# A transformer layer's value projection: its second phase moved behind the fourth pair of the step, a weighting product in its old place

## What is computed

```python
q, k, v = proj(Wq, bq), proj(Wk, bk), proj(Wv, bv)        # (B, 16, S, 16), v as 256 features
q = _apply_rope(q, cos, sin) * scale
k = _apply_rope(k, cos, sin)
attn = jax.nn.softmax(jnp.einsum('bhsd,bhtd->bhst', q, k), axis=-1)
out = jnp.einsum('bhst,bhtd->bhsd', attn, v)
x = _layernorm(x + out @ Wo.T + bo)
h = jax.nn.relu(x @ Wq1.T + b1)                           # Wq1, Wq2 in {-1, 0, 1}
x = _layernorm(x + h @ Wq2.T + b2)
```

## Time and profile before

| | us |
|---|---|
| median of 3 runs | 3234.84 (3234.15 to 3235.83) |
| the profiled execution | 3235.67 |
| its span, first to last instruction | 3233.9 |
| TensorE busy | 3190.5 |
| VectorE busy | 2970.8 |
| ScalarE busy | 2528.2 |
| GpSimd busy | 2157.4 |
| mean granted TensorE clock | 0.991 |

### The profile page before, as it was taken

How to read it: one execution, slowest core, us unless ns; L and a number is a source line. 1 busy time by engine, 2 the same in 40 slices (tenths; PEclk the granted TensorE clock), 3 DMA queues, 4 the chain that set the end, 5 groups by cost and what they waited for, 6 DMA issues and landing times.

```text
span 3233.9 us, 82328 instructions
## 1 busy us (share of the span) xinstructions
PE 3190.5 (99%) x31110; PEld 1769.4 (55%) x31110; DVE 2970.8 (92%) x5710; ACT 2528.2 (78%) x4963; POOL 2157.4 (67%) x2457
## 2 busy tenths in 40 slices
PE   6999999999999999999999999999999999999998
PEld 4545555555555555555555555555555555555555
DVE  7989999999999999999999999999999999999993
ACT  3878888878888888878878877888878878877774
POOL 2676766766766766766767767767767667664455
PEclk7999999999999999999999999999999999999999
DMA  8445354454354454454454454454453453453411
GB/s 214 115 102 110 92 118 106 99 118 110 94 119 107 98 119 105 100 119 99 103 119 103 100 119 102 103 119 100 105 119 96 106 121 91 111 110 73 97 57 35
DMA packets 312712, 342.02 MB, mean 106 GB/s; under 512 B 77372, under 2 KB 259964, under 8 KB 312316
## 3 DMA queue, kind: packets, MB, share of 16 engines
q1 hardware_dynamic: 311740, 335.97, 45.5%
q10 hardware_dynamic: 576, 0.79, 0.2%
HBM read 196.41 MB, written 140.24 MB: 104 GB/s over the span
## 4 chain that ended last, share of the span: by engine, by line
PE 97%; DMA 1%; ACT 1%; DVE 1%; issue 0%; SPq 0%; POOL 0%; ACTq 0%; POOLq 0%; DVEq 0%
PE ob L1049 31%; PE sc L1031 27%; PE job L787 26%; PE ms L1019 11%; PE job L838 0%; ACT prob L1187 0%; PE ms L895 0%; DVE mxp L1619 0%; PE sc L787 0%; DMA qa<-qk_parts 0%; SPq L482 0%; ACT at_st L1194 0%; DMA maxima<-nm 0%; DMA attention<-at_st 0%; DMA os_<-wv 0%
## 5 line engine op out<-in xcount | busy, mean ns | idle before, releaser
L1367 DVE TENSOR_REDUCE mxp<-ms 128x1 f32<-128x512 f32 x4064 | 2602.2, 680 | 193.3 <-PE ms L1019 155.8
L1187 ACT ACTIVATE prob<-sc 128x512 f32<-128x512 f32 x4096 | 2224.9, 597 | 593.7 <-PE sc L1031 562.0
L1019 PE MATMUL ms<-ka,qa 48*128 48x512 f32 x4064 | 1494.4, 440 | 3.3 <-DVE mxp L1619 2.2
L1031 PE MATMUL sc<-qa,ka 50*128 50x512 f32 x4096 | 1495.0, 438 | 2.2 <-ACT prob L1187 0.8
L1031 PEld LDWEIGHTS sc<-qa,ka 50*128 50x128 f32 x4096 | 694.3, 184 | 1020.9 <-ACT prob L1187 862.4
L1049 PE MATMUL ob<-prob,v_sb 128*17 128x512 f32 (+1 forms) x8528 | 1087.3, 582 | 4.5 <-ACT at_st L1194 4.2
L1019 PEld LDWEIGHTS ms<-ka,qa 48*128 48x128 f32 x4064 | 692.7, 184 | 11.7 <-DVE mxp L1367 5.2
L1735 POOL TENSOR_TENSOR ve<-mv,eps_sb 128x2 f32<-128x2 f32 x123 | 24.1, 196 | 571.9 <-DVE mv L1394 571.9
L1756 POOL TENSOR_TENSOR hid_r<-hid,hid_r 128x512 fp32r<-128x512 f32 x248 | 319.6, 1289 | 19.8
L1049 PEld LDWEIGHTS ob<-prob,v_sb 128*17 128x17 f32 x8528 | 141.4, 95 | 314.1 <-issue 314.0
L787 PEld LDWEIGHTS job<-h_t,w_sb 64*128 64x128 f32 x3968 | 271.4, 185 | 17.8 <-issue 1.6
(11 more groups left out here) (251 smaller groups left out, 2740.4 us busy)
## 6 DMA issues: line engine op xcount, KB each, us to landing
qk_parts<-parts SPq DMA_DIRECT2D x122, 512.0 KB, 4.3
ka<-qk_parts SPq DMA_DIRECT2D x378, 128.0 KB, 4.7
qa<-qk_parts SPq DMA_DIRECT2D x378, 128.0 KB, 7.3
attention<-at_st SPq DMA_DIRECT2D x127, 256.0 KB, 4.1
v_sb<-v_ones SPq DMA_DIRECT2D x68, 272.0 KB, 8.4
v_ones<-v_st SPq DMA_DIRECT2D x64, 272.0 KB, 2.4
xn<-x SPq DMA_DIRECT2D x63, 256.0 KB, 4.7
out<-y SPq DMA_DIRECT2D x63, 256.0 KB, 3.9
```

What stands on the lines that cost most here:

```text
L1019: nc.tensor.matmul(ms[upto(b, g, NS1, at) % MS_BANKS][:, :], operand(qa, b, unit_, j, ROWS)[:, qt * P:(qt + 1) * P], operand(ka, b, unit_, ...
L1031: nc.tensor.matmul(sc[upto(b, g, HG * STEPS, n) % SC_BANKS][:, :], operand(ka, b, unit_, j, ROWS + MROWS)[:, tt * P:(tt + 1) * P], operand ...
L1187: nc.scalar.activation(prob[st_ % 2][:, j, :], sc[upto(b, g, HG * STEPS, n) % SC_BANKS][:, :], ACT.Exp).then_inc(s["exp_done"], 1)
L1367: nc.vector.reduce_max(mxp[(b * G + g) % 2][:, kh, j * TT + qt:j * TT + qt + 1], ms[upto(b, g, NS1, at) % MS_BANKS][:, :], AX.X).then_inc( ...
```

## The change

`"v1"` joins the tuple of jobs that stand behind the fourth pair. So TensorE issues the product of the step before behind the second pair, and `v1` behind the fourth. ScalarE's copy of `v1` goes from between the second and third exponential to behind the fourth, and VectorE's copy from behind the second maximum to behind the third.

```diff
-JOBS_BEHIND = ("e0", "o0", "v0", "t3a", "f0", "f2", "g0", "g2")
+JOBS_BEHIND = ("e0", "o0", "v0", "v1", "t3a", "f0", "f2", "g0", "g2")
...
                         for job_ in jobs_at(b, g, st_, tail):
-                            finish(job_)
+                            if job_[2] != "v1":
+                                finish(job_)
...
                         for job_ in jobs_at(b, g, st_, tail):
+                            if job_[2] == "v1":
+                                finish(job_)
                             finish_rest(job_)
...
-                                if stage == "proj" and part == 1:
+                                if stage == "proj" and part == (2 if name == "v1" else 1):
                                     take_key_half(*at, name)
```

## The result

| | before | changed |
|---|---|---|
| median of 7 runs, us | 3235.01 (3234.15 to 3236.9) | 3245.57 (3243.6 to 3249.24) |
| the profiled execution, us | 3235.67 | 3249.24 |
| its span, us | 3233.9 | 3247.4 |
| mean granted TensorE clock | 0.991 | 0.991 |

The changed kernel is slower: ratio 1.0032, 95% interval 1.0022 to 1.0041, 10.6 us between the medians. 3245.7 us was predicted, 3238 to 3252 as the range. The profiled execution of the changed kernel is the slowest of its seven, so its span is 13.5 us longer where the medians differ by 10.6. I therefore compare steps, which repeat, and not ends.

What follows compares the result with a forecast made beforehand. TensorE, busy 99%, was taken to bound the kernel, held up by ScalarE's exponential latency. 8.6 + 1.0 + 1.3 = 10.9 us on 3235.67 gave 3246.6; less 0.8 for the median, 3245.7 us, range 3238 to 3252.

Steps and rivals of the forecast that it cites:

- Steps 7 and 8: TensorE's two steps with `v1` and `f0`: 3.09 and 3.32 us, together 6.41 us against 6.25 before.
- All eight distances: Starts between pairs: step 7 0.40, 1.41, 0.34, 0.94 us; step 8 0.39, 1.41, 0.34, 1.18 us.
- 0.16 us per unit: Extra time of steps 7 and 8 in each of 54 units, 8.6 us in all.
- The copies cost nothing: ScalarE's and VectorE's moved copies of `v1`: nothing counted; ScalarE's margins 0.5 and 0.3 us at step 8's third and fourth pairs.
- VectorE's margin at step 8's third pair: Fourth tile's maximum ends about 2.5 us after step 7's third pair; the pair reusing its bank stands at 3.07 us.
- Batch 0: Six places at 0.16 us, 1.0 us in all; in two, `split_x` queues behind the late copy, 0.64 us each, 1.3 us.
- the late load is paid: Rival: late load costs nothing at a product; steps 7 and 8 6.19 us, about 3234 us in all; chance 0.10.
- The exponentials did not come sooner: Rival: ScalarE, relieved of the copy, serves step 7's last tiles earlier; gain 0.19 us 54 times, about 3225 us; chance 0.04.
- No queue tipped over: Rival: VectorE or ScalarE falls behind by more than its margin; 0.1 to 0.2 us more per unit, 3251 to 3257; chance 0.08.
- the waits of weight loads for `sc` grow: Sign in the list of waits: those for `sc`, 862.4 us before, grow; those for `ms` stay near 5 us.

Runs made afterwards that it cites:

- its control on the kernel before: Kernel before, with the exponential of step 7's fourth tile cut to 128 of 512 columns in 52 units: 3235.03 us, ratio 1.0.
- the late and the small copy: Changed kernel, two runs: VectorE's copy of `v1` behind the fourth maximum, 3246.43 us, ratio 1.0038; ScalarE's copy cut to a quarter, 3248.45 us, ratio 1.0041.
- two_short_exps_after: Changed kernel with the exponentials of step 7's third and fourth tiles cut to 128 of 512 columns in 52 units: 3235.57 us against 3234.66, ratio 1.0003.
- short_exp_after: Changed kernel with the exponential of step 7's fourth tile cut to 128 of 512 columns in 52 units: 3237.77 us against 3236.27, ratio 1.0004.
- three edits: Changed kernel, step 7's third and fourth exponentials cut to 128 columns in 52 units, VectorE's `v1` copy behind the fourth maximum: 3230.95 us against 3235.0, ratio 0.999.
- more_after: Changed kernel with four more matmuls in `v1` (16 instead of 12) for 56 units: 3246.89 us, ratio 1.0034.
- more_before: Kernel before with four more matmuls in `v1`, which stands behind the second pair there: 3241.49 us, ratio 1.0019.
- f0_mid: Changed kernel with `f0` taken back behind the second pair of step 8: 3258.79 us, ratio 1.0076.

## Why the prediction was right, point by point

- *Steps 7 and 8, 3.09 + 3.32 = 6.41 us:* measured 3.09 and 3.33 us in the median. All eight distances are within 0.01 us of the terms in the median. The mechanism, the wait of step 8's second pair for the fourth exponential, is shown by the cut on the changed kernel with its control on the kernel before, and by the added matmuls, of which the wait took up 0.17 of 0.23 us.
- *0.16 us per unit:* 0.18 us from the 9.3 us of 52 units. With batch 0 that makes 11.8 us by steps, where 10.9 were reckoned and the medians differ by 10.6. That the median came within 0.2 us of the forecast is luck: the interval of the ratio alone spans 7 to 13 us.
- *The copies cost nothing:* right in the units with a tail, by the late and the small copy. VectorE's margin at step 8's third pair is 0.59 us, as reckoned (a maximum that ends at 2.5 us, a pair at 3.07). I had overlooked the fourth pair, which needs the next maximum: there it is only 0.10 us. In `two_short_exps_after`, where the pairs come 0.28 us sooner, it is used up. In batch 0 VectorE's copy does cost something, the 0.4 us above; my 0.16 us for each of these places did not contain it.
- *Batch 0, 1.0 + 1.3 = 2.3 us:* from the steps that hold the six places and the two steps behind each I read 2.1 us. The two with `split_x` cost 0.57 and 0.59 us (I had 0.80 each), the two at step 13 0.17 and 0.19, the two at step 7 0.29 each. The exponential that stands behind both copies and holds its pair is seen there.
- *The rivals:* the product behind a late pair took 1.41 us, so the late load is paid. The rule of the Trainium skill ("TensorE: Matmul & The Clock Gate", "Step-by-step: what each phase is for"), that weight loads are pulled ahead of matmuls in flight if their rows don't conflict or the background buffer takes them, would hide them all if no semaphore were in the way. The trace agrees for a pair behind a pair or a job whose exponential is done (step 8's fourth pair in the changed kernel: load at 1613.98, matmul at 1614.21), not for a load that waits for an exponential, and not for the first load behind a product, which starts with its own matmul (1610.77 and 1610.78). The exponentials did not come sooner: ScalarE was idle for 0.73 us before them, so relieving it of a copy bought nothing. No queue tipped over.
- *The sign "the waits of weight loads for `sc` grow":* it came true, but not for my reason, and proves nothing. I had read the 862.4 us of the earlier trace rows as waits for exponentials. Of them 767.7 us stand before loads behind a product, and only 94.7 us before others. Those grew by 4.4 us only, since one wait went where another came. The sum did not rest on this row.
- *What I had missed, without effect on the sum:* under the wait I priced there are two more, which cost 0.05 and 0.06 us per unit once it is gone. In `short_exp_after` I therefore expected 3232 us and measured 3237.8.

## What to carry to other kernels

When one engine is busy 99% and still waits, count from start to start between the instructions that share a buffer, and give each filler the latency it has to cover. Here the third pair of a step and the second pair of the next are tied by score, exponential and semaphore: 1.68 us in the changed kernel (1610.78 to 1612.46), where I had taken 1.66 from `e0`'s step. What stands between the two, if it is shorter than that, is paid for as if it had that length, so short jobs belong where the wait is already paid. If a job moves, its copies must move with it on every engine, to a place where nothing that is needed sooner queues behind them. And a wait that goes may uncover the next: three edits were needed before the order itself showed its price. A list of waits by releaser can mislead: before you count a wait, look whether the named instruction had ended long before.

## What the runs showed of the hardware

A weight load that has to wait for its exponential costs about 0.10 us more than one that doesn't, in the distance to what follows: a product starts 0.43 instead of 0.33 us after the pair, a job 0.34 instead of 0.23, in the medians of batches 1 to 13 of both kernels, and of `short_exp_after`, `two_short_exps_after`, `more_after`, `more_before` and `f0_mid`. The record of its matmul is 0.50 instead of 0.39 us. I had read that from one pair. But 0.50 us in a record is not the mark of a semaphore: a pair right behind a product has it too, though its exponential had ended 0.58 us (1603.73) or 0.68 us (1610.77) before.

New to me was what the first pair of step 8 does, which has a second semaphore to wait for (that of the loaded maxima). In the changed kernel, `short_exp_after` and `f0_mid` its load starts 0.11 us after the end of its exponential, behind a separate semaphore instruction of 0.05 us, where a load with one semaphore starts 0.05 us after. So it is late even when it misses its exponential by little.
